# GpSimd's routing sends paced by steps of other engines, a key-query product moved to VectorE, and solving steps spread differently

## The reference, cut to what matters

```
x = x + linear_attention(layernorm(x))        # 16 heads of 64, relu features, normalized by k_sum
x = x + ffn(layernorm(x))                     # first expert layer
x = x + layer_norm(h + delta_memory(h) @ w_o.T)   # h = layernorm(x); fast-weight memory over 8 steps
x = x + ffn(layernorm(x))                     # second expert layer

def ffn(h):                                   # 8 experts, 512 hidden
    g = softmax(h @ Wr); top2_w, top2_idx = top_k(g, 2); top2_w /= sum(top2_w)
    expert_out = relu(h @ W1[e]) @ W2[e]      # for every expert e
    return sum of the two chosen experts' outputs, times top2_w
```

## Time and profile before

| | |
|---|---|
| median of 3 runs | 1131.63 us (1125.02 to 1134.97) |
| the profiled execution | 1121.75 us, of it 1120.0 us from first to last instruction |
| TensorE busy | 967.3 us (86%) |
| VectorE, ScalarE, GpSimd busy | 539.4, 541.3, 378.5 us |
| mean granted TensorE clock | 0.933 |
| linear attention; first experts; memory; second experts | to 310; 310 to 480; 480 to 893; 893 to 1120 us |

### The profile page before, as it was taken

The page is one execution under the profiler, slowest core; times in us unless marked ns, Lnnn a source line. Parts: engine busy times, 40 slices in busy tenths (PEclk is TensorE's granted clock), DMA queues, the critical chain, the costliest instruction groups (busy, mean ns, idle before and its releaser), DMA issues.

```text
span 1120.0 us, 31388 instructions
## 1 busy us (share of the span) xinstructions
PE 967.3 (86%) x11919; PEld 724.6 (65%) x11919; DVE 539.4 (48%) x1908; ACT 541.3 (48%) x1082; POOL 378.5 (34%) x391
## 2 busy tenths in 40 slices
PE   7999999999897699969987998898889887557990
PEld 6455666656697699945445745754576787557990
DVE  4246535544562322155695687368767564130103
ACT  2444343343043355537666666646646454225770
POOL 2201233222245565530412012331332254455551
PEclk9999999999897899989999999989989898788995
DMA  8633432134031232050202100201071211112316
GB/s 219 177 78 78 94 96 65 43 90 91 25 80 51 75 83 64 29 151 4 77 3 76 42 21 23 92 15 50 21 229 46 52 52 42 48 51 74 86 35 227
DMA packets 83506, 82.75 MB, mean 74 GB/s; under 512 B 12335, under 2 KB 64388, under 8 KB 82848
## 3 DMA queue, kind: packets, MB, share of 16 engines
q1 hardware_dynamic: 68864, 58.30, 20.0%
q0 software_dynamic: 10176, 19.04, 5.4%
q10 hardware_dynamic: 4320, 3.41, 1.1%
HBM read 53.96 MB, written 27.64 MB: 73 GB/s over the span
## 4 chain that ended last, share of the span: by engine, by line
PE 32%; DVE 8%; issue 6%; ACT 5%; another core or an unknown queue 2%; POOL 1%; DMA 1%; SPq 0%; ACTq 0%; POOLq 0%; DVEq 0%
PE b_ring L1717 6%; PE b_ring L1282 6%; PE b_ring L1271 5%; PE b_g L1761 4%; PE b_g L1736 3%; PE b_ring L1684 2%; ACT early L1881 2%; PE b_ring L1776 2%; DVE b_kq L2114 2%; DMA early<-expert_parts 1%; ACT b_outT L1893 1%; POOL b_last_pair L1573 1%; DVE b_outT L110 1%; DVE b_prod L2030 1%
## 5 line engine op out<-in xcount | busy, mean ns | idle before, releaser
L1717 PE MATMUL b_ring<-b_hT,b_qkT 128*128 128x512 f32 x256 | 120.7, 609 | 6.0 <-DVE b_kq L2114 5.9
L1282 PE MATMUL b_ring<-wide,b_v 128*128 x568 | 81.3, 289 | 26.8 <-issue 16.1
L2114 DVE SCALAR_TENSOR_TENSOR b_kq<-b_exp,b_ring 128x512 f32<-128x512 f32 x128 | 83.1, 683 | 39.8 <-ACT b_exp L1867 38.5
L1271 PE MATMUL b_ring<-b_v,b_kq 128*128 128x128 f32 x568 | 81.2, 289 | 16.5 <-issue 11.1
L276 POOL DMA_INDIRECT expert_rows<-f_route_sent,f_route_place_id x64 | 62.0, 969 | 94.9 <-DVE f_route_place_id L232 50.9
L1282 PEld LDWEIGHTS b_ring<-wide,b_v 128*128 128x128 f32 x568 | 74.2, 204 | 28.3 <-issue 28.1
L1271 PE MATMUL a_ring<-phik 128*128 128x128 f32 x568 | 78.7, 284 | 12.9 <-ACT phik L1292 11.9
L1867 ACT ACTIVATE b_exp<-b_ring 128x512 f32<-128x512 f32 x128 | 73.5, 604 | 31.9 <-PE b_ring L1717 20.1
L1271 PEld LDWEIGHTS b_ring<-b_v,b_kq 128*128 128x128 f32 x568 | 74.4, 204 | 18.9 <-issue 12.5
L1717 PEld LDWEIGHTS b_ring<-b_hT,b_qkT 128*128 128x128 f32 x256 | 45.2, 189 | 62.2 <-issue 37.6
L1282 PE MATMUL a_wide<-wide,phiqT 128*128 x568 | 78.4, 283 | 5.6 <-ACT phiqT L1297 3.5
(11 more groups left out here) (331 smaller groups left out, 1906.4 us busy)
## 6 DMA issues: line engine op xcount, KB each, us to landing
a_rn_wide<-norm_compact SPq DMA_DIRECT2D x28, 512.0 KB, 10.1
wide<-in_L_ffn_W SPq DMA_DIRECT2D x32, 256.0 KB, 6.1
a_rn_wide<-expert_rows SPq DMA_DIRECT2D x71, 65.0 KB
b_coef<-gram_compact SPq DMA_DIRECT2D x4, 1024.0 KB, 4.9
early<-expert_parts SPq DMA_DIRECT2D x16, 256.0 KB, 5.1
b_hT<-expert_rows SPq DMA_DIRECT2D x56, 65.0 KB
x<-in_L_attn_a_x SPq DMA_DIRECT2D x8, 256.0 KB, 4.3
early<-expert_parts SPq DMA_DIRECT2D x4, 512.0 KB, 5.9
```

The costliest lines, as they stand in the source:

```text
L1271: ins = pe.matmul(self.hid_bank[j % 2][:, f * P:(f + 1) * P], self.w1_now[:, b % W1_SLOTS, f * P:(f + 1) * P], self.blkT[:, b % HID_SLOTS, ...
L1282: ins = pe.matmul(self.y_bank[j % 2][:, 0:P], self.hidT[:, b % HID_SLOTS, f, :], self.C["w2"][:, bass.ds(e, 1), f, :].rearrange("p a c -> ...
L1717: pe.matmul(ring[n % 4][:, :], w, hT[:, g % 2, half * 512:half * 512 + 512], start=True, stop=True)\
L2114: dve.scalar_tensor_tensor(out=kq[:, p % 2, half:half + FOURS // 2, slot:slot + T * FOUR], in0=exps[:, n % EXPS, :].rearrange("p (a n) -> ...
```

## The change

Every row of eight sends that ran without waits gets some. In the last batch of attention: `pace_last`. In the first expert layer routes 6 and 7 are sent one a block, after scatters 10 to 17 and 18 to 25. In the memory, routes 0, 2 and 3 wait for steps of mixing and of the values that follow, route 1 goes in twos between the pairs of group 3. Route 4 waits for hidden blocks, and its last five sends alternate with the first scatters; routes 5, 6 and 7 go one a block after scatters 7 to 14, 16 to 23 and 24 to 31. The last pair of each group is multiplied by VectorE (`end_pair`, own semaphore `pair_ended`). The solving lists, two steps in group 0 and one order in the tail of VectorE are moved.

```diff
+        def pace_last(i):
+            if i == 1:
+                return kv_done, 3 * LAST + 3
+            if i == 3:
+                return norm_done, LAST + 1
+            if i in (5, 7):
+                return spread_done, (i - 3) // 2
+            return y_done, NT * (LAST - 1) + i // 2 + 1
...
-                    if i and t < LAST:
-                        sem, count = pace(t, i)
+                    if i:
+                        sem, count = pace(t, i) if t < LAST else pace_last(i)
                         wait_apart(pool, sem, count, K.passed)
                     router.send_one(pool, t - 2, i)
...
                 ffn.scatter(pool, j)
                 if j == 1:
                     router.root(pool, LAST)
-                elif j == 10:
-                    route_slot(LAST - 1)
-                    router.send(pool, LAST - 1)
-                elif j == 16:
-                    route_slot(LAST)
-                    router.send(pool, LAST)
+                for r, first in ((LAST - 1, 10), (LAST, 18)):
+                    if first <= j < first + 2 * NT:
+                        route_slot(r)
+                        router.send_one(pool, r, j - first)
...
-            pair_lasts(0, 0, 7)
+            pair_lasts(0, 0)
             ln.root(pool, C["minus_half"], 2)
-            pair_last(0, 7)
...
-            send(0)
-            ln_out.root(pool, C["minus_half"], 1)
+            for i in range(2 * NT):
+                sem, count = (S["mixed_full"], 16 + 10 + 2 * i) if i < 3 else (S["v_full"], 32 + 1 + 3 * (i - 3))
+                wait_apart(pool, sem, count, K.passed)
+                router.send_one(pool, route(0), i)
+                if i == 4:
+                    ln_out.root(pool, C["minus_half"], 1)
             shift(3)
-            for i in range(2 * NT):
-                router.send_one(pool, route(1), i)
-                if i >= 4 and i % 2 == 0:
-                    pair_last(3, i // 2 - 2)
-            pair_lasts(3, 2, 5)
+            for p in range(NT):
+                pair_last(3, p)
+                router.send_one(pool, route(1), 2 * p)
+                wait_apart(pool, S["kq_full"], 32 * 3 + 4 * p + 7, K.passed)
+                router.send_one(pool, route(1), 2 * p + 1)
+            pair_last(3, 4)
...
-            send(2)
+            for i in range(2 * NT):
+                sem, count = (S["mixed_full"], 32 + 12 + 2 * i) if i < 2 else (S["v_full"], 48 + 1 + 5 * (i - 2) // 2)
+                wait_apart(pool, sem, count, K.passed)
+                router.send_one(pool, route(2), i)
             ln_out.root(pool, C["minus_half"], 2)
             for i in range(2 * NT):
                 if i == NT:
                     root(4)
+                wait_apart(pool, S["mixed_full"], 48 + 3 + i, K.passed)
                 router.send_one(pool, route(3), i)
             for i in range(2 * NT):
-                if i == NT:
+                if i == 2:
                     root(5)
+                elif i == 4:
                     ln_out.root(pool, C["minus_half"], 3)
+                if i:
+                    wait_apart(pool, ffn.F["hid_done"], ffn.first + i, K.passed)
                 router.send_one(pool, route(4), i)
-            for j in range(BLOCKS):
+                if i >= 3:
+                    ffn.scatter(pool, i - 3)
+            for j in range(2 * NT - 3, BLOCKS):
                 ffn.scatter(pool, j)
-                if j == 1:
+                if j == 6:
                     root(6)
-                elif j == 3:
-                    for i in range(2 * NT):
-                        if i == NT:
-                            root(7)
-                        router.send_one(pool, route(5), i)
-                elif j == 8:
-                    send(6)
-                elif j == 15:
-                    send(7)
+                elif j == 11:
+                    root(7)
+                for r, first in ((5, 7), (6, 16), (7, 24)):
+                    if first <= j < first + 2 * NT:
+                        router.send_one(pool, route(r), j - first)
...
-                    pe.wait_ge(S["last_paired"], PAIRS * g + p + 2)
+                    if p < PAIRS - 1:
+                        pe.wait_ge(S["last_paired"], (PAIRS - 1) * g + p + 2)
+                    else:
+                        pe.wait_ge(S["pair_ended"], g + 1)
...
-            BEFORE = {1: 1, 2: 11, 3: 9}
-            BESIDE = {1: (2, 4, 6, 8, 10, 11, 12, 13, 14, 15, 16, 17, 18, 19, 20), 2: (1, 4, 6, 8, 10),
-                      3: (1, 3, 4, 6, 8, 9, 10)}
+            BEFORE = {1: 1, 2: 11, 3: 7}
+            BESIDE = {1: (3, 5, 7, 9, 10, 11, 12, 13, 14, 15, 16, 17, 18, 19, 20), 2: (1, 4, 6, 8, 10),
+                      3: (1, 3, 4, 6, 8, 9, 10, 12, 13)}
...
-                    if g == 0 and n == 12:
+                    if g == 0 and n == 11:
                         add_parts(1)
-                    if g == 0 and n == 26:
+                    if g == 0 and n == 19:
                         statistics(1)
...
+                dve.wait_ge(S["kq_ready"], g * 32 + 32)
+                end_pair(g)
                 if g > 0:
                     build(g - 1, 0)
...
             place(4)
+            residual(3)
             route_statistics(5)
-            residual(3)
```

More of the change, by code:

```diff
@@ L1412, in delta_memory @@
                  "gram_stored0", "gram_stored1", "coef_loaded", "mix_ready", "mix_stored", "tok_loaded", "own_step", "spread_built", "late_built", "last_paired",
-                 "mixed_full", "outT_ready", "att_done", "att_read", "normed", "scaled", "shifted", "x_ready", "parts_added"]
+                 "pair_ended", "mixed_full", "outT_ready", "att_done", "att_read", "normed", "scaled", "shifted", "x_ready", "parts_added"]
         S = {n: K.sem(f"b_{n}") for n in names}
@@ L1575, in pair_last, with pair_lasts @@
                     .then_inc(S["last_paired"], 1)
-            def pair_lasts(g, first, end):
+            def pair_lasts(g, first, end=PAIRS - 1):
                 for p in range(first, end):
@@ L1608, in _ @@
             shift(1)
-            pair_lasts(1, 0, PAIRS)
+            pair_lasts(1, 0)
             store_products(pool, 1, 1)
@@ L1617, in _ @@
             root(1)
-            pair_lasts(2, 6, PAIRS)
+            pair_lasts(2, 6)
             store_products(pool, 2, 1)
-            send(0)
-            ln_out.root(pool, C["minus_half"], 1)
-            shift(3)
-            for i in range(2 * NT):
-                router.send_one(pool, route(1), i)
-                if i >= 4 and i % 2 == 0:
-                    pair_last(3, i // 2 - 2)
-            pair_lasts(3, 2, 5)
+            for i in range(2 * NT):
[4 more added lines that the diff above has]
+                    ln_out.root(pool, C["minus_half"], 1)
+            shift(3)
+            for p in range(NT):
[4 more added lines that the diff above has]
+            pair_last(3, 4)
             root(2)
@@ L1630, in _ @@
             root(3)
-            pair_lasts(3, 6, PAIRS)
+            pair_lasts(3, 6)
             store_products(pool, 3, 1)
-            send(2)
+            for i in range(2 * NT):
+                sem, count = (S["mixed_full"], 32 + 12 + 2 * i) if i < 2 else (S["v_full"], 48 + 1 + 5 * (i - 2) // 2)
+                wait_apart(pool, sem, count, K.passed)
+                router.send_one(pool, route(2), i)
             ln_out.root(pool, C["minus_half"], 2)
@@ L2104, in route_normalize, with end_pair @@
                 router.normalize(dve, route(r))
+            def end_pair(g):
+                key, query = KEYS + (T - 1) * FOUR, QUERIES + (T - 1) * FOUR
+                dve.tensor_tensor(last_pair[:, 1, :].rearrange("p (a b) -> p a b", b=FOUR),
+                                  kq[:, 1, :, key:key + FOUR], kq[:, 1, :, query:query + FOUR], ALU.mult)\
+                    .then_inc(S["pair_ended"], 1)
             def keys_and_queries(g):
```

## The result

The changed kernel takes 1084.36 us (median of 4 runs, 1078.89 to 1085.49) against 1128.83 for the kernel before on the same chip: ratio 0.959, 95% interval 0.954 to 0.964. Its profiled execution took 1078.89 us, 42.9 less than the one of before.

The account below looks back on a forecast made before the run. TensorE was taken to bound the kernel, busy 967 of 1120 us. Gains of 28 us up to the second expert layer without the first, plus 38 in the expert layers, made 66: 1131.63 - 66 = 1066 us, range 1034 to 1110.

Parts of the forecast that it names:

- the expert layers: Both expert layers: sends paced one a block cut the loss from 81 us, a gain of 38 (bounds 3 and 78).
- The premise: Rows of sends: a run of transfers starves the engines of instructions after some 5 us; an inference from eleven stretches.
- Rival (c): Whole kernel: stalls only stand beside the runs, the waits change nothing, only 8 us remain: 1124 us; chance 0.11.
- Last batch: Last batch of attention: paced sends bring the normalizer group back to about 2 us; gain 8.6 us (bounds 3 and 9.5).
- routes 2 and 3: Memory's third and last mixing: route 2 gains 3.5 of 8 us, the matrix's DMA being late next; route 3 gains 2.5.
- Route 0: Second mixing and values: 10.2 us lost, three sends still together in mixing charged 0.98 us each; gain 7 us.
- The last pair: Last product of a group, moved from GpSimd to VectorE: gain 1.9 us in each of groups 1 to 3, 5.7.
- Group 0, route 1: Memory: group 1's later root and two moved steps gain 0.4 us; route 1's sends in twos lose 1.3 in group 3.
- T = 3.2 a block: Expert layers: a block with scatter and send takes 3.2 us, at 1.6 per transfer (bounds 2.56 and 3.8).
- reserve: Five expert-layer rows: a run costs nothing for its first 4.8 us, so each row loses 8 us instead of 10.5.
- Rival (a): Expert layers: rows gain nothing, total transfers being the same; loss again about 80 us, time 1104 us; chance 0.20.
- The barrier of block 40: Second expert layer: block 40's fetch waits for route 7's last send, with 2 us of cover; price 0, up to 4.

Follow-up runs that it names:

- second pair: The kernel before and the changed kernel, neither altered, executed once more each on another chip: 1124.03 us before, ratio 0.965 for the changed kernel.
- probes: Changed kernel plus useless indirect DMAs in both expert layers (one a block, a run of eight, one in two blocks) and eight GpSimd products: 1124.96 us, ratio 0.997.
- second trace: The changed kernel, not altered, run again on a chip where the kernel before takes about 1130 us: 1087.97 us, ratio 0.965.
- first variant: Changed kernel with routes 6 and 7 of the first expert layer sent as rows of eight again: 1025.22 us against 1020.58 for the kernel before, ratio 1.0034.

## Why the prediction was right or wrong

**Direction and range were right, the size was not.** 66 us were forecast; 42.9 came in the profiled executions (44.5 in the medians), and 35.6 in the second pair. Outside the expert layers 20 of 28 us came, in them 21 of 38 (17 and 18 in the second pair). The term that was sized most wrongly is that of the expert layers.

**The premise was right on stalling chips and only there.** The probes put transfers alone beside a TensorE that lost nothing, and it lost 13.3 us for eight in a run. Rival (c) is false there. On a smooth chip, as (c) has it, the waits change nothing. I had argued from "twelve runs and no gap of that size without one"; that a trace is of one chip was not in the argument, and the result was measured on a chip of the same kind as the trace.

**Last batch, routes 2 and 3: right.** 8.3 for 8.6, 3.7 for 3.5, 3.0 for 2.5 (7.8, 4.9 and 5.0 in the second pair). In the last batch the eight sends now start 1.95 us apart on average instead of 1.27. That it is the waits is read from the lengths of these stages; the waits were taken out only on a smooth chip, where they are worth nothing. The give-back of route 2 came as forecast: the mixing ahead gained 8.6 us, and the wait for the DMA behind `build(3, 0)` took 4.9 of it back.

**Route 0: right once (7.6 for 7), not the second time (1.1).** The three sends left in mixing were charged 1 us each. The term lacked the clock: in the second trace part of the stretch ran at half speed. Why it did so there and not in the first is not shown.

**The last pair: wrong step.** "TensorE waited 2.40 us for it" was read as 1.9 us to win. The next release was already close behind: ScalarE's copy of earlier products ends 0.4 us ahead of GpSimd's product. Measured 0.3 to 0.6 instead of 1.9 a group. It could have been read in group 0 of the trace before, where no `build` slows GpSimd and the same products wait for ScalarE:

```profile
537.92 1.48 PE L1736 MATMUL b_g<-b_kq 64*32 64x64 f32 x128 [1.35 <-ACT wide L1859]
```

**Group 0, route 1: small losses.** Moving the two steps and the root, forecast as a gain of 0.4, came out as a loss of 1.4 and 0.4 over both groups. Group 3 lost 2 us net; -1.3 and +1.9 had been forecast.

**The expert layers: the rate was right, the credit wrong.** T = 3.2 a block was forecast, 3.06 to 3.44 measured. The failing step is "a loss of 10.5 less some reserve, 8 a row, because a run costs nothing for its first 4.8 us". The loss was 9.4 to 14 a row, 59 us instead of 40, and route 4 kept 5.7 us where 2.5 stood (3.0 in the second trace). There is no reserve that each row gets anew: the loss goes with the number of transfers beyond one a block, 1.1 to 1.9 us for each. Rival (a) had the reason (the total of transfers is the same) and is nearly what the first layer did, which gained 2.5 and 1.0 us. The second layer's gain came mostly (12 of 17 us) from another part of the edit, by the traces from rows that no longer stand behind a late place number.

**The barrier of block 40: price 0 on the stalling chip was right, for another reason.** The feedback kept GpSimd level with TensorE. On a smooth chip it is 8 to 10 us. The cover had been worked out for route 7 alone; the backlog of routes 5 and 6 stands in front of it.

**What was to be seen.** L858 at 2 us and the wait before the last pair: yes. Over 110 matmuls per 20 us: 316/58 x 20 = 109 in the first layer, 468/82.1 x 20 = 114 in the second. GpSimd waiting for place numbers with scatters behind: gone. No gap above 3 us in rows of sends: wrong, 3.49 and more remain.

## What to carry to other kernels

When an engine's wait is removed, the gain is the distance to the next release that is due on the same instruction, not the length of the wait; look for a sister place in the trace where the second release is already the last. If a loss follows a kind of operation, measure its price by adding eight useless ones where nothing is lost, singly and in a run, before spreading the real ones. Pacing helped here where there was room: in the last batch, with no other transfers, it won 8 us. Where each block already had its own transfer, spreading the same number over the same blocks won 1 to 2.5 us in the first layer and 5 in the second. And run the kernel before on more than one chip: a change tuned to one chip's stalls was worth 3.5 to 4% there, while its variants stood 0.1 to 0.5% behind on another.

## What the runs showed of the hardware that was not expected

The same kernel takes 1128.9 us on some chips and 1020.6 on others. Between the changed kernel's trace and that of its first variant on a smooth chip (1078.9 and 1025.6 us) 47 of the 53 us lie in the two expert layers. On the stalling chips each transfer beyond one a block costs TensorE 1.1 to 1.9 us, partly as a stall of all other engines at once, partly as half clock after it; on the smooth ones 43 in 58 us cost nothing. GpSimd's own time is the same on both (0.98 busy, 0.30 idle), and so is the instruction queue's share. Instruction supply was my theory; a sequence of small matmuls with no wait in it is held too, in gaps of 0.4 us, which speaks for it. Against it speaks that 13.3 us were lost with no instruction packet under way but one at the start of the stretch. How the engines are held is thus open: a late signal between engines was not excluded, nor was a cause named that tells the two kinds apart. Open as well: the changed kernel itself was not run on a smooth chip, nor the kernel before traced there, so how far the 8 to 10 us at block 40 are new is argued, not shown.
